# Cross-attention inside a two-layer decoder: the next context is requested at head 5 of a batch, and the totals are inverted in two halves at heads 11 and 13

## The chip, the cores and the metric

The kernel runs as one program on one core of a Trainium2 chip. Its time is the device time of one execution in microseconds (us). Three executions of the kernel before took 2054.67, 2056.34 and 2062.97 us, so the median is 2056.34 us. Five engines work side by side: TensorE (PE, with its weight loads shown apart as PEld), VectorE (DVE), ScalarE (ACT), GpSimd (POOL) and SyncE (SP), which here only issues DMAs. The 16 DMA engines of the core serve every queue.

## The reference, cut to what matters

The decoder has two layers. The change touches only the cross-attention of layer 0: 16 batches, 112 queries and 375 context rows each, 16 heads of width 16.

```python
q = x @ Wq + bq
kv = context @ Wkv + bkv
k, v = jnp.split(kv, 2, axis=-1)
# 16 heads of 16; both q and k are rotated by position
q = _larope(q, Lq)
k = _larope(k, Lk)
scores = jnp.einsum('bhqd,bhkd->bhqk', q, k) * SCALE
scores = jnp.where(context_mask[:, None, None, :], scores, -jnp.inf)
attn = jax.nn.softmax(scores, axis=-1)
out = jnp.einsum('bhqk,bhkd->bhqd', attn, v)
out = out.transpose(0, 2, 1, 3).reshape(B, Lq, H * hd)
return out @ Wo + bo
```

## The kernel before, in words

Every engine has its own instruction list, written by hand, and waits on semaphores. In the cross-attention stage each list is a loop over batches `b` and, inside a batch, over heads `h` from 0 to 15. Where a step stands in that loop fixes its place in its engine's order. `ahead(b, s, h + n, step)` runs a step for a head n places later, running over into the next batch; `s` is the parity of the batch and picks one of two buffers.

What one batch needs:

- **The context** of batch b+3 (375 KB) is loaded into one of three buffers by `load_context`, issued from ACT's queue. Before the change this happens in `copy_values`, at the third value copy, which stands at head 15. The buffer's last readers are the value matmuls (`values`, L1582), counted by `v_ready`.
- **Keys.** PE projects the keys of batch b+2 from its context at heads 0, 1, 2 and 4 (`keys`, L1571). DVE rotates them at heads 2, 3, 5, 6 (L1691), POOL adds and subtracts, and ACT casts three bf16 parts at heads 8, 12 and 14 (`cast_keys`, L1781). SP stores each part to DRAM (`store_parts`, L1444, 187.5 KB each). Then SP loads them back in the layout of the score matmul (`load_keys`, L1474): four loads of 187.5, 375, 562.5 and 375 KB; the last two wait for the third part's store. PE needs them for the first score of batch b+2, which stands at head 10 of batch b+1, since `scores` runs six heads ahead.
- **Scores and weights.** PE computes `scores(h+6)` (L1592), DVE biases them and takes their minimum, `bias_scores(h+4)` (L1703), ACT exponentiates, `exponentiate(h+3)` (L1786), PE transposes, `turn_probs(h+2)` (L1602), and DVE (L1709) or ACT (L1792) copies the result, `copy_probs(h+1)`. There are three buffers of scores, so `scores(n)` waits for `bias_scores(n-3)`. Every four heads PE weighs the values (L1618).
- **Totals.** The values' tile holds columns of ones, so the weighing gives the weighed sums and the total weights. ACT copies them at head 1 of the next batch (`copy_sums`, L1797), SP moves them with four DMAs (`move_sums`, L1483), which go behind `load_keys` on the same queue, DVE inverts the totals at head 12 (`invert`, L1714, semaphore `inverted`), and POOL multiplies (`scale_sums`, L1542).

In the first batches two more things run: ACT casts queries (L1817) and SP stores them (`store_queries`, L1454), in front of `move_sums`.

Of the kernel before, what the change touches and what calls it, by code (L numbers as in the profile page):

```python
# [24 lines left out]
B, L, D = 16, 112, 256  # L25
T = B * L
DH = D // P
# [1250 lines left out]
def cross_attention(k, g, ins):  # L1278
# [12 lines left out]
    with ExitStack() as ctx:  # L1291
# [27 lines left out]
        CK = S2 // KC  # L1319
# [4 lines left out]
        with ExitStack() as c2:  # L1324
# [20 lines left out]

            KEYS_AT, ROTATE_AT, CAST_AT = (0, 1, 2, 4), (2, 3, 5, 6), (8, 12, 14)
            VALUES_AT, COPY_VALUES_AT = (8, 9, 10, 11, 12, 13), (11, 13, 15)
            TURNED_BY_ACT = (1, 3, 5, 7, 8, 9, 11, 13, 15)
            TURNED_BY_DVE = tuple(h for h in range(NHEAD) if h not in TURNED_BY_ACT)

# [29 lines left out]
            def follows(b, n=1):  # L1380

                return not isinstance(b, int) or b + n < B

            def precedes(b):
                return not isinstance(b, int) or b > 0
# [47 lines left out]
            def load_context(queue, b):  # L1433
                queue.dma_start(context_of(b), ins["ctxT"][ds(b, 1)].rearrange("b (h p) t -> p (b h) t", p=P)).then_inc(ctx_loaded[b % len(contexts)], 16)
# [76 lines left out]
            @block.gpsimd  # L1511
            def _(pool):
                def sum_keys(b):
                    pool.wait_ge(k_read, b + 1)

                    wait(pool, k_cast, PARTS * b)
                    pool.tensor_tensor(key[:, 0], turn[:, 0], turn[:, 2], ALU.subtract)
                    pool.tensor_tensor(key[:, 1], turn[:, 1], turn[:, 3], ALU.add).then_inc(k_whole, 1)

                def lessen_keys(b, n):  # L1520

                    pool.wait_ge(k_cast, PARTS * b + n + 1)
                    pool.tensor_tensor(key[:], key[:], part[:, n], ALU.subtract).then_inc(k_less, 1)

                def lessen_queries(g_no, n):
                    pool.wait_ge(q_cast, PARTS * (g_no - 1) + n + 1)
                    pool.tensor_tensor(query_both(g_no), query_both(g_no), query_part(g_no, n), ALU.subtract).then_inc(q_less, 1)

                def turn_queries(g_no):

                    pool.wait_ge(q_kept, g_no - OTHERS)
                    for n, table in enumerate((q_cos, q_sin, q_sin, q_cos)):
                        last = pool.tensor_tensor(by_length(turned_query(g_no, n)), by_length(query(g_no, n // 2)), over_batches(table, g_no), ALU.mult)
                    last.then_inc(q_turned, 1)
                    pool.wait_ge(q_turned, g_no - OTHERS)
                    pool.tensor_tensor(query(g_no, 0), turned_query(g_no, 0), turned_query(g_no, 2), ALU.subtract)
                    pool.tensor_tensor(query(g_no, 1), turned_query(g_no, 1), turned_query(g_no, 3), ALU.add).then_inc(q_whole, 1)

                def scale_sums(b, s):

                    pool.wait_ge(inverted, b + 1)
                    pool.tensor_tensor(merged[:, :, chunk(b, L)], value_sum[:, s], power_sum[:, s], ALU.mult).then_inc(o_scaled, 1)  # L1542

                pool.memset(v[:], 1.0).then_inc(v_filled, 1)
                sum_keys(1)
                pool.wait_ge(q_whole, 2)
                for n in range(PARTS - 1):
                    lessen_keys(1, n)
                    lessen_queries(OTHERS, n)
                for b in range(B - 2):  # L1550
                    if b < NCH - 1:
                        turn_queries(OTHERS + 1 + b)
                    sum_keys(b + 2)
                    for n in range(PARTS - 1):
                        if b < NCH - 1:
                            lessen_queries(OTHERS + 1 + b, n)
                        lessen_keys(b + 2, n)
                    if b > 0:
                        scale_sums(b - 1, (b - 1) % 2)
                for b in range(B - 3, B):  # L1560
                    scale_sums(b, b % 2)
# [120 lines left out]
            def _(dve):  # L1682
# [25 lines left out]
                    dve.wait_ge(t_ready, NHEAD * b + h + 1)  # L1708
                    dve.tensor_copy(pt[:, h % PT_RING], turned_probs(h)).then_inc(pt_ready[0], 1)  # L1709

                def invert(b, s):

                    dve.wait_ge(o_moved[s], 16 * 4 * (b // 2 + 1))
                    dve.reciprocal(power_sum[:, s], power_sum[:, s]).then_inc(inverted, 1)  # L1714

                def batch(b, s):
                    for h in range(NHEAD):
                        ahead(b, s, h + 4, bias_scores)
                        if (h + 1) % NHEAD in TURNED_BY_DVE:
                            ahead(b, s, h + 1, copy_probs)  # L1720
                        if h == 12 and precedes(b):
                            invert(b - 1, 1 - s)
                        if follows(b, 2) and h in ROTATE_AT:
                            rotate_keys(b + 2, ROTATE_AT.index(h))

# [31 lines left out]
                    bias_scores(0, 0, h)  # L1757
                copy_probs(0, 0, 0)
                batches(dve, batch)
                invert(B - 1, 1)  # L1760

            @block.scalar
            def _(act):
                def copy_values(b, s, c):
                    if c == 0:

                        wait(act, pv_done, QUADS * (b - 1))
                    act.wait_ge(v_ready, CK * b + c + 1)
                    if c == CK - 1 and follows(b, 3):

                        load_context(act, b + 3)
                    act.activation(v[:, s, c, :, 0::2], value_ps(c).rearrange("p (h d) -> p h d", d=HD), ACT.Copy).then_inc(v_read, 1)

                def cast_keys(b, n):
# [19 lines left out]
                def copy_sums(b, s):  # L1794
                    act.wait_ge(pv_done, QUADS * (b + 1))
                    wait(act, o_moved[s], 16 * 4 * (b // 2))
                    act.activation(o_sb[:, s], o_ps[:, 0:QUADS * L].rearrange("p (r l) -> p r l", l=L), ACT.Copy).then_inc(o_copied, 1)  # L1797
# [28 lines left out]
                def batch(b, s):  # L1826
                    for h in range(NHEAD):
                        ahead(b, s, h + 3, exponentiate)
                        if b < NCH - 1 and h in CAST_QUERIES_AT:
                            cast_queries(OTHERS + 1 + b, CAST_QUERIES_AT.index(h))  # L1830
                        if (h + 1) % NHEAD in TURNED_BY_ACT:
                            ahead(b, s, h + 1, copy_probs)
                        if h == 1 and precedes(b):
                            copy_sums(b - 1, 1 - s)
                        if follows(b, 2) and h in CAST_AT:
                            cast_keys(b + 2, CAST_AT.index(h))
                        if follows(b) and h in COPY_VALUES_AT:
                            copy_values(b + 1, 1 - s, COPY_VALUES_AT.index(h))
# [1691 lines left out]
```

## Time and profile before

| | |
|---|---|
| median of three executions | 2056.34 us |
| the profiled execution's own time | 2056.47 us |
| its span | 2054.6 us |
| TensorE clock, mean of what was granted | 0.949 of full speed |
| PE busy | 1773.9 us, 86% |
| DVE busy | 1418.9 us, 69% |
| ACT busy | 1045.2 us, 51% |
| POOL busy | 1002.3 us, 49% |

The profile gives times in microseconds from the start of the span. A matmul is shown by its modelled end, so a full PE is not a PE at its peak. The loop over the batches of the cross-attention lies between about 533 and 822 us of the span; one batch takes some 17.5 us there once it runs evenly, and up to 21 us in the first ones.

### The profile page before, as it was taken

How to read it: one execution, taken by the hardware profiler on the slowest of the kernel's cores; microseconds unless marked ns; L12 is line 12 of the kernel's file. 1: busy time of each engine (PE TensorE's matmuls, PEld its weight loads, DVE VectorE, ACT ScalarE, POOL GpSimd, SP SyncE). 2: the span in 40 equal slices, each digit the busy share in tenths (PEclk: the TensorE clock that was granted, in tenths of full speed). 3: DMA queues.
4: the chain of work that ended last, by engine and by line, in shares of the span. 5: the costliest groups of instructions: out<-in, count | busy, mean ns of one | idle time of the engine just before them, and what ended most of it. 6: DMA issues, size and time to landing. Idle time of an engine off the chain costs nothing. (4 is left out here: it accounts for less than half of the span.)

```text
span 2054.6 us, 33436 instructions
## 1 busy us (share of the span) xinstructions
PE 1773.9 (86%) x11006; PEld 1107.5 (54%) x11006; DVE 1418.9 (69%) x2635; ACT 1045.2 (51%) x1948; POOL 1002.3 (49%) x756
## 2 busy tenths in 40 slices
PE   7967887889989999787888888888689989999799
PEld 4334444445667777443444444444554656665699
DVE  6779999993678888495555555554565348787893
ACT  4776667661788888336555554554323131114342
POOL 1269989881653321036566666665100009764342
PEclk9979999999999999899999989999899999999899
DMA  2034334433687774411556544633940044344640
GB/s 70 5 117 134 126 126 138 122 99 108 144 184 185 187 184 103 126 40 31 178 151 201 177 141 147 197 98 72 294 136 0 1 138 144 113 138 147 223 139 17
DMA packets 147377, 261.12 MB, mean 127 GB/s; under 512 B 39877, under 2 KB 104038, under 8 KB 144534
## 3 DMA queue, kind: packets, MB, share of 16 engines
q1 hardware_dynamic: 129846, 216.22, 35.7%
q0 software_dynamic: 13824, 37.77, 6.0%
q10 hardware_dynamic: 3536, 4.99, 0.9%
q8 instruction: 90, 1.47, 0.3%
q14 instruction: 81, 0.66, 0.1%
HBM read 205.82 MB, written 49.44 MB: 124 GB/s over the span
## 5 line engine op out<-in xcount | busy, mean ns | idle before, releaser
L3128 POOL DMA_INDIRECT moe_y<-ahead,moe_where x144 | 159.9, 1110 | 141.2 <-DVE ahead L3261 112.0
L3191 PE MATMUL moe_up_ps<-moe_w_tile,ahead 128*64 128x352 f32 x1152 | 214.3, 521 | 2.8 <-ACT moe_w_tile L3335 1.4
L2335 POOL TENSOR_TENSOR soft_power<-soft_logit,soft_high 128x1024 f32<-128x1024 f32 x28 | 66.2, 2363 | 289.3 <-DVE soft_high L2409 289.0
L3335 ACT ACTIVATE moe_w_tile<-moe_w 128x1216 f32 x144 | 175.4, 1219 | 24.1 <-issue 21.9
L3122 POOL DMA_INDIRECT ahead<-moe_tok,moe_where x144 | 144.2, 1001 | 56.9 <-issue 42.7
L1786 ACT ACTIVATE xattn_prob<-xattn_sm,xattn_least 112x375 f32<-112x375 f32 x256 | 150.8, 604 | 29.1 <-DVE xattn_least L1703 28.6
L1023 POOL TENSOR_TENSOR mamba_x_state<-mamba_x_state,mamba_cx_all 128x896 f32<-128x896 f32 x64 | 133.4, 2085 | 26.8 <-DVE mamba_x_state L1081 26.8
L3191 PEld LDWEIGHTS moe_up_ps<-moe_w_tile,ahead 128*64 128x64 f32 x1152 | 85.7, 153 | 103.1 <-issue 93.5
L1017 POOL TENSOR_TENSOR xn<-mamba_u,mamba_b_all 128x896 f32<-128x896 f32 x64 | 133.3, 2086 | 14.7 <-DMA mamba_b_all<-mamba_b 14.7
L1703 DVE CUSTOM_DVE_ANT_0 xattn_sm<-xattn_s_ps,wide 112x375 f32<-112x375 f32 x256 | 130.2, 539 | 13.0 <-PE xattn_s_ps L1592 9.7
L3255 DVE TENSOR_TENSOR moe_hid<-ahead,moe_up_ps 128x176 f32<-128x176 f32 x144 | 45.7, 333 | 133.9 <-ACT ahead L3341 82.5
L1081 DVE TENSOR_TENSOR_SCAN mamba_x_state<-xn,mamba_x_in 128x896 f32<-128x896 f32 x64 | 128.7, 2011 | 4.6 <-PE mamba_x_in L1116 4.6
L1602 PE MATMUL xattn_pt_ps<-ident,xattn_prob 112*125 112x112 f32 x768 | 126.7, 274 | 5.9 <-ACT xattn_pt L1792 3.8
L1602 PEld LDWEIGHTS xattn_pt_ps<-ident,xattn_prob 112*125 112x125 f32 x768 | 113.9, 189 | 31.5 <-issue 14.0
L1121 PE MATMUL mamba_y<-mamba_x_state,ident 128*128 128x448 f32 x256 | 108.1, 545 | 16.4 <-POOL mamba_x_state L1023 16.3
L980 ACT ACTIVATE mamba_scaled<-wide,mamba_b_turned 128x256 f32<-128x256 f32 x224 | 95.8, 495 | 48.7 <-PE mamba_x_in L1116 47.8
L3112 DVE COPY moe_w_tile<-moe_w 128x1216 f32 x144 | 109.1, 799 | 11.6 <-issue 11.6
L1121 PE MATMUL mamba_y<-ahead_small,ident 128*128 128x448 f32 x256 | 107.8, 544 | 0.0
L2359 PE MATMUL soft_lg<-soft_phi,xn 128*128 128x512 f32 x224 | 102.3, 600 | 4.4 <-PEq L365 4.4
L1116 PE MATMUL mamba_x_in<-ident,mamba_scaled 128*128 128x128 f32 x448 | 63.0, 282 | 49.6 <-ACT mamba_scaled L980 35.7
L2444 ACT ACTIVATE soft_power<-soft_power 128x1024 f32<-128x1024 f32 x28 | 29.6, 1058 | 149.1 <-POOL soft_power L2335 149.1
L2370 PE MATMUL soft_mix<-soft_tok,soft_share 128*128 128x256 f32 x448 | 101.2, 380 | 2.5 <-POOL soft_share L2340 1.3
(458 smaller groups left out, 4273.8 us busy)
## 6 DMA issues: line engine op xcount, KB each, us to landing
moe_w<-moe_w SPq DMA_DIRECT2D x64, 480.0 KB
soft_w<-soft_w SPq DMA_DIRECT2D x16, 1024.0 KB, 7.4
mamba_b_all<-mamba_b SPq DMA_DIRECT2D x32, 448.0 KB
mamba_cx_all<-mamba_c SPq DMA_DIRECT2D x32, 448.0 KB, 3.7
mamba_cy_all<-mamba_c SPq DMA_DIRECT2D x32, 448.0 KB, 4.5
moe_w_tile<-moe_y SPq DMA_DIRECT2D x14, 1024.0 KB, 8.1
soft_logits<-soft_logit SPq DMA_DIRECT2D x28, 512.0 KB, 2.6
soft_logit<-soft_logits SPq DMA_DIRECT2D x14, 1024.0 KB, 5.1
```

The costliest lines, as they stand in the source:

```text
L1017: pool.tensor_tensor(y_in[:, j % 2], u[:, c0 + j % 2, tok], b_all[:, n % 2], ALU.mult).then_inc(y_fed, 1)
L1023: pool.tensor_tensor(x_state[:, j % 2], x_state[:, j % 2], cx_all[:, n % 2], ALU.mult).then_inc(x_read, 1)
L1081: dve.tensor_tensor_scan(x_state[:, j % 2], x_decay[:, j % 2], x_in[:, 0:HW], 0.0, ALU.mult, ALU.add).then_inc(x_scanned, 1)
L1121: mm = pe.matmul(y[:, j % 2, w, 0:CW], g.ident[:], src[:, j % 2, w * CW:(w + 1) * CW], start=False, stop=False, skip_group_check=True)
L1602: mm = pe.transpose(turned_probs(h)[:, c], prob[:, h % RING, c * KC:(c + 1) * KC], g.ident[0:L, 0:L])
L1703: dve.tensor_tensor_reduce(sm[:, h % RING], s_ps[0:L, (NHEAD * b + h) % S_RING, 0:S2], mask[:, s], -SCALE, BIG, ALU.add, ALU.min, least[:, ...
L1786: act.activation(prob[:, h % RING], sm[:, h % RING], ACT.Exp, bias=least[:, s, h:h + 1], scale=-1.0).then_inc(p_ready, 1)
L3112: copy(w_tile[:, s, i, n:n + 1].rearrange("p a m -> p (a m)"), w[:, ds(e & (RING - 1), 1)].rearrange("p a m -> p (a m)")).then_inc(w_place ...
L3122: pool.indirect_dma_start(xg[:, 2 * s + i], None, tok_dram, bass.IndirectOffsetOnAxis(ap=where[:, 0, t:t + 1], axis=0)).then_inc(gathered[ ...
L3128: pool.indirect_dma_start(y_dram, bass.IndirectOffsetOnAxis(ap=where[:, 1, t:t + 1], axis=0), y_sb[:, 2 * s + i], None).then_inc(y_stored[ ...
L3191: mm = pe.matmul(up_ps[n * HALF:(n + 1) * HALF, i, 0:2 * I], xT[:, s % 2, at:at + HALF], w_tile[:, s, i, n, h * 2 * I:(h + 1) * 2 * I], st ...
L3335: place_weights = weight_placer(act, 0, lambda to, src: act.activation(to, src, ACT.Copy))
```

## The change: what it does

Two edits, both in the cross-attention.

1. The request for the context of batch b+3 leaves `copy_values` (head 15 of batch b-1, behind a cast of the keys) and stands at head 5 of batch b. In front of it ACT waits for all three value products of batch b, which were made in batch b-1. The load itself, its queue and its size stay.
2. The inversion of the totals becomes two operations on half of the columns each, one at head 11 and one at head 13, where one operation stood at head 12. The first half waits for the four DMAs of `move_sums`. `inverted` now counts two per batch, and POOL waits for both. After the last batch both halves follow one another.

```diff
+            CONTEXT_AT, INVERT_AT = 5, (11, 13)
...
-                    pool.wait_ge(inverted, b + 1)
+                    pool.wait_ge(inverted, DH * (b + 1))
...
-                def invert(b, s):
-
-                    dve.wait_ge(o_moved[s], 16 * 4 * (b // 2 + 1))
-                    dve.reciprocal(power_sum[:, s], power_sum[:, s]).then_inc(inverted, 1)
+                def invert(b, s, m):
+
+                    if m == 0:
+                        dve.wait_ge(o_moved[s], 16 * 4 * (b // 2 + 1))
+                    dve.reciprocal(power_sum[:, s, m], power_sum[:, s, m]).then_inc(inverted, 1)
...
-                        if h == 12 and precedes(b):
-                            invert(b - 1, 1 - s)
+                        if h in INVERT_AT and precedes(b):
+                            invert(b - 1, 1 - s, INVERT_AT.index(h))
...
-                invert(B - 1, 1)
+                for m in range(DH):
+                    invert(B - 1, 1, m)
...
-                    if c == CK - 1 and follows(b, 3):
-
-                        load_context(act, b + 3)
...
+                        if h == CONTEXT_AT and follows(b, 3):
+
+                            act.wait_ge(v_ready, CK * (b + 1))
+                            load_context(act, b + 3)
```

The line numbers below L1345 grow by one in the changed kernel. On DVE, heads 11 to 14 of one batch, before the change. ISA is the biasing of one head's scores with its minimum, COPY a `copy_probs`, TENSOR_SCALAR the next batch's mask, RECIPROCAL the inversion:

```order
L1709 COPY xattn_pt<-xattn_pt_ps 125x336
L1697 TENSOR_SCALAR wide<-ahead 112x375
L1703 ISA xattn_sm,xattn_least<-xattn_s_ps,wide 112x375
L1703 ISA xattn_least 112x1
L1714 RECIPROCAL ahead_small<-ahead_small 128x224
L1703 ISA xattn_sm,xattn_least<-xattn_s_ps,wide 112x375
L1703 ISA xattn_least 112x1
L1709 COPY xattn_pt<-xattn_pt_ps 125x336
```

The same place on DVE after the change:

```order
L1710 COPY xattn_pt<-xattn_pt_ps 125x336
L1716 RECIPROCAL ahead_small<-ahead_small 128x112
L1698 TENSOR_SCALAR wide<-ahead 112x375
L1704 ISA xattn_sm,xattn_least<-xattn_s_ps,wide 112x375
L1704 ISA xattn_least 112x1
L1704 ISA xattn_sm,xattn_least<-xattn_s_ps,wide 112x375
L1704 ISA xattn_least 112x1
L1710 COPY xattn_pt<-xattn_pt_ps 125x336
L1716 RECIPROCAL ahead_small<-ahead_small 128x112
```

The inversion, and with it the wait for the moved sums, now stands ahead of the mask and of the biasing of the next batch's first head; its second half follows the copy of head 14.

On ACT, heads 14 and 15 before the change. ACTIVATE `xattn_part` is the last key cast, `xattn_prob` an exponential, `xattn_v` the third value copy:

```order
L1781 ACTIVATE xattn_part<-xattn_key 128x750
L1786 ACTIVATE xattn_prob<-xattn_sm,xattn_least 112x375
L1434 DMA ahead<-ctxT 128x2x375
L1772 ACTIVATE xattn_v<-xattn_kv_ps 125x256
L1786 ACTIVATE xattn_prob<-xattn_sm,xattn_least 112x375
```

And on ACT after the change, heads 1 to 6 of the next batch, where ACTIVATE `ahead_small` is `copy_sums`:

```order
L1797 ACTIVATE ahead_small<-xattn_o_ps 128x448
L1786 ACTIVATE xattn_prob<-xattn_sm,xattn_least 112x375
L1792 ACTIVATE xattn_pt<-xattn_pt_ps 125x336
L1786 ACTIVATE xattn_prob<-xattn_sm,xattn_least 112x375 x2
L1792 ACTIVATE xattn_pt<-xattn_pt_ps 125x336
L1786 ACTIVATE xattn_prob<-xattn_sm,xattn_least 112x375
L1435 DMA ahead<-ctxT 128x2x375
L1786 ACTIVATE xattn_prob<-xattn_sm,xattn_least 112x375
L1792 ACTIVATE xattn_pt<-xattn_pt_ps 125x336
```

The request has moved from just behind the last key cast to the exponential at head 5.

## Rows read from the trace of the kernel before

**Rows 1.** Engines by stretch (busy us, count), TensorE clock, DMA share, GB/s.
```profile
core 0: us, PE busy (x) PEld busy (x) DVE busy (x) ACT busy (x) POOL busy (x), PEclk, DMA share, GB/s
650.00:670.00 20.00, 19.60 (x216) 15.25 (x217) 16.67 (x53) 17.86 (x40) 5.39 (x5) 1.00 0.82 198
```

**Rows 2.** Who waited for whom, 533 to 829: total us, times, longest.
```profile
DVE ahead_small L1714 <- DMA ahead_small<-ahead_small: 10.7, 4, 5.7
...
PE xattn_s_ps L1592 <- DVE xattn_least L1703: 7.6, 17, 2.0
...
PE xattn_s_ps L1592 <- DMA xattn_ks<-xattn_k_parts: 6.9, 9, 1.3
```

**Rows 3.** DMA issues in time, end of batch 11: start, duration, queue, line.
```profile
755.32 0.37 ACTq L1434 DMA_DIRECT2D ahead<-ctxT  x1
756.16 0.36 SPq L1444 DMA_DIRECT2D xattn_k_parts<-xattn_part  x1
760.22 0.77 SPq L1474 DMA_DIRECT2D xattn_ks<-xattn_k_parts  x2
```

**Rows 4.** DMA issues in time, end of batch 12, which requests no context.
```profile
774.59 0.36 SPq L1444 DMA_DIRECT2D xattn_k_parts<-xattn_part  x1
778.01 0.77 SPq L1474 DMA_DIRECT2D xattn_ks<-xattn_k_parts  x2
```

**Rows 5.** DMA view, 755 to 761: issue, count, KB, us to landing.
```profile
xattn_k_parts<-xattn_part SPq DMA_DIRECT2D x1, 187.5 KB, 4.0
```

**Rows 6.** The same view, 774.5 to 779.
```profile
xattn_k_parts<-xattn_part SPq DMA_DIRECT2D x1, 187.5 KB, 3.3
```

**Rows 7.** TensorE in time: first scores of three batches, with their idle time.
```profile
768.53 0.37 PE L1592 MATMUL xattn_s_ps<-xattn_ks,xattn_qs 128*112 128x375 bf16 x1 [1.27 <-DMA xattn_ks<-xattn_k_parts]
786.29 0.37 PE L1592 MATMUL xattn_s_ps<-xattn_ks,xattn_qs 128*112 128x375 bf16 x1 [0.61 <-DMA xattn_ks<-xattn_k_parts]
803.29 0.37 PE L1592 MATMUL xattn_s_ps<-xattn_ks,xattn_qs 128*112 128x375 bf16 x1 [1.14 <-DMA xattn_ks<-xattn_k_parts]
```

**Rows 8.** DMA view, 533 to 829: ACT's queue (packets, MB, share), then one issue.
```profile
q10 hardware_dynamic: 3264, 4.61, 6.0%
...
ahead<-ctxT ACTq DMA_DIRECT2D x8, 375.0 KB, 3.5
```

**Rows 9.** VectorE in time, batch 2, around the inversion.
```profile
587.20 0.79 DVE L1697 TENSOR_SCALAR wide<-ahead 112x375 f32<-112x375 uint8 x1
588.20 0.55 DVE L1703 CUSTOM_DVE_ANT_0 xattn_sm<-xattn_s_ps,wide 112x375 f32<-112x375 f32 x1 [0.21 <-DVE wide L1697]
590.76 1.55 DVE L1714 RECIPROCAL ahead_small<-ahead_small 128x224 f32<-128x224 f32 x1 [2.00 <-DMA ahead_small<-ahead_small]
592.23 0.49 DVE L1703 CUSTOM_DVE_ANT_0 xattn_sm<-xattn_s_ps,wide 112x375 f32<-112x375 f32 x1
```

**Rows 10.** TensorE in time: scores around the inversions of batches 1 to 3.
```profile
571.81 0.37 PE L1592 MATMUL xattn_s_ps<-xattn_ks,xattn_qs 128*112 128x375 bf16 x1 [0.94 <-DVE xattn_least L1703]
...
588.76 0.32 PE L1592 MATMUL xattn_s_ps<-xattn_ks,xattn_qs 128*112 128x375 bf16 x1
...
589.68 0.32 PE L1592 MATMUL xattn_s_ps<-xattn_ks,xattn_qs 128*112 128x375 bf16 x1
...
592.78 0.37 PE L1592 MATMUL xattn_s_ps<-xattn_ks,xattn_qs 128*112 128x375 bf16 x1 [2.02 <-DVE xattn_least L1703]
...
613.04 0.37 PE L1592 MATMUL xattn_s_ps<-xattn_ks,xattn_qs 128*112 128x375 bf16 x1 [1.63 <-DVE xattn_least L1703]
```

**Rows 11.** Instruction groups by shape: busy us, mean ns, idle before.
```profile
L1714 DVE RECIPROCAL ahead_small<-ahead_small 128x224 f32<-128x224 f32 x16 | 24.8, 1549 | 10.7 <-DMA ahead_small<-ahead_small 10.7
...
L506 DVE RECIPROCAL xattn_proj_out_ln_rstd<-xattn_proj_out_ln_rstd 128x112 f32<-128x112 f32 x4 | 3.4, 853 | 2.5 <-ACT xattn_proj_out_ln_rstd L502 2.5
```

**Rows 12.** Engines by stretch, batch 2, columns as in rows 1.
```profile
576.00:586.00 10.00, 9.51 (x96) 7.13 (x94) 8.37 (x27) 8.52 (x18) 6.29 (x6) 1.00 1.05 214
```

**Rows 13.** ScalarE in time, heads 3 to 6 of one even batch.
```profile
708.54 1.11 ACT L1786 ACTIVATE xattn_prob<-xattn_sm,xattn_least 112x375 f32<-112x375 f32 x2 [0.46 <-DVE xattn_least L1703]
```

## The prediction

> **What bounds the kernel now.** I read the engines by stretch first. In the even part of the cross-attention PE is busy 19.60 of 20 us, at the full granted clock, while the DMA engines are at 0.82 [rows 1]. So PE is nearly full; ACT and DVE follow at 17.86 and 16.67, and no change of order there can return more than PE's small holes. The list of waits names the holes: PE waited 6.9 us in nine places for the keys coming back from DRAM, and 7.6 us in 17 places for DVE's biased scores [rows 2]. Together that is 14.5 us, 0.7% of the span. Nothing in the diff lowers the work of PE, so this is the ceiling of a gain, and I look at each of the two holes by itself.
>
> The hole for the keys is a chain of DMAs: the third part is cast at head 14, stored, and only when it has landed do the last two loads go out; the first score of the next batch but one waits for them. In the batch that ends at 756 the store goes out at 756.16, the last loads at 760.22 [rows 3], and the score starts at 768.53 after 1.27 us idle [rows 7]: 12.37 us from store to score.
>
> The hole for DVE is mostly in batches 1 to 3. There the inversion waits for the moved sums: 2.00 us in batch 2 [rows 9]. The next biasing starts 592.23, and PE's score behind it at 592.78, after 2.02 us idle; batches 1 and 3 show 0.94 and 1.63 [rows 10]. These three are 4.6 of the 7.6 us.
>
> **The change part by part.** All is summed against the profiled execution's own time, 2056.47 us (1.9 above its span), which is 0.13 above the median of 2056.34.
>
> *The context request, what it leaves.* Before, it goes out 0.84 us ahead of the third store (755.32 against 756.16) [rows 3] and shares the DMA engines with it. Batch 12 asks for no context and is a control: its store lands in 3.3 us, where the one behind a context took 4.0 [rows 5, 6], the last loads follow after 3.42 us instead of 4.06, and store to score is 11.70 us (774.59 to 786.29) instead of 12.37 [rows 3, 4, 7]. So leaving this place is worth 0.67 us on the keys' chain.
>
> *Where it arrives.* At head 5 the ACT queue reaches it with the exponential that starts at 708.54 [rows 13] in a batch whose keys PE takes up near head 10, 5 us on. The keys' loads are then under way. One context costs 6.0% of 296 us over 12 requests, 1.48 us of all 16 engines [rows 8]. If all of it goes ahead of the last key, the keys are 1.48 us later. If the engines turn evenly between the two queues, much of it is left over when the keys are through, and at a share of 0.82 [rows 1] some 0.9 us of the 5 are free and take a part too, so that the cost may be near 0. The net on the keys' chain is then between -0.67 and +0.81 us per batch. I take the middle, a cost about equal to the 0.67 saved, and so zero; both ends stay for the range. There are nine even batches with a context (4 to 12): -6.0 to +7.3 us. PE feels a loss fully, since it already waits for the keys in most batches, and a gain only as far as it waits.
>
> ACT's added wait, for the values of this batch, is for products made in the batch before, so it holds nothing up; behind it are the exponential of head 9 and a copy. The context is used at head 0 of the next batch, 11 heads or some 12 us later, and a context lands in 3.5 us [rows 8]: hidden even if that triples.
>
> *The inversion in halves.* One operation of 128x224 takes 1.549 us, one of 128x112 0.853 [rows 11]; two are 1.71, so 0.16 us more per batch on DVE. DVE has 3 us and more free in 20 [rows 1], so in the middle this costs PE little; after the last batch nothing covers it: +0.16 us. What is better is that no block is longer than 0.85; against it, in even batches, the mask and first biasing of the next batch come 0.8 us later. Scores are made three ahead of the biasing, which is about one head, 0.92 us (588.76 to 589.68) [rows 10]. So this is covered with 0.1 us to spare if the sums have landed. Of 16 inversions only four wait today [rows 2], at head 12. At head 11 some more will, by 0 to 0.5 us. I take 0, with an upper bound of 0.4 x 9 = 3.6.
>
> *The inversion in batches 1 to 3.* Here the sums are late whatever DVE does, and the order decides. Let the sums land at L. Before, the biasing for the next batch's head 0 was done while waiting (588.20) [rows 9], and PE stood at the following score but one, which began at L + 2.02 (590.76 to 592.78). Now the mask and this biasing stand behind the first half: 0.85 + 0.79 + 0.21 + 0.55 [rows 9, 11], 2.4 us less 0.1 where operations overlap (the biasing at 592.23 starts 0.08 before the reciprocal's end at 592.31). The earlier score starts at L + 2.3 and the one that PE stood at one head later, L + 3.2. That is 1.2 us more in each, 3.6 us in three batches.
>
> L itself moves. From 576 to 586, where the context of head 5 now falls, the DMA engines are saturated (1.05) [rows 12], and the sums go out behind everything. The context adds its 1.48 us there; leaving its old place gives back what it held up there, 0.67, or 0.9 if all of its overlap is counted. I take +0.6 us each, 1.8 in all.
>
> Sum: 3.6 + 1.8 + 0.16 + 0 = +5.6 us, so 2056.5 + 5.6 = 2062.1; rounded 2062.
>
> **The rivals.**
>
> *Absorbed.* The three early stalls lie in batches where ACT also casts queries; a later wait takes up what is lost, and the keys' chain nets zero. For it: in such a batch ACT is busy 8.52 of 10 us and PE 9.51 [rows 12], so that a later stall could be behind ACT and not behind this one. Against: PE is idle exactly for DVE there [rows 10]. Time 2056.5.
>
> *Faster.* The saving of 0.67 us counts, and the context slips in beside the keys for nothing; the smaller blocks on DVE also spare PE its short waits. The nine waits for keys, 6.9 us [rows 2], fall: at 0.67 x 9 = 6.0 us, 2050.5. Against it: in batch 12, without any context, PE still waits 0.61 us, and the last one 1.14 [rows 7], so the waits do not go away when contention does.
>
> *Slower, past the bound.* The context goes ahead of the keys whole. The keys' chain is then 1.48 - 0.67 = 0.81 us longer in nine batches, +7.3, on top of the 5.6: 2069.4. It decides once a context holds up the keys by more than 0.67 us. For it: the DMA engines are at 0.8 already, and PE stands at the keys with no slack. It is the one that the skill's rule would make true.
>
> *The change does not do what it says.* The request could be held at head 5 by its new wait; the counts exclude it, and I give it nothing.
>
> **How the numbers follow.** Forecast 48%, absorbed 18%, faster 14%, slower past the bound 20%. The forecast's own range is 2057 to 2067. The range of 2051 to 2069 leaves out about half of the gain case and half of the slow one. A measurement of this kernel can tell about 0.5%, 10.3 us, from no change: faster means under 2046.1, which only an excess over the gain case reaches, 4%. Slower means over 2066.6: three quarters of the slow case and a tail of the forecast, 19%. The rest, 77%, is the same.
>
> **What would show each step.** In the profile after: the third store landing in about 3.3 us in every batch and the last loads 3.4 us behind it (leaving); the waits of the first scores for `xattn_ks`, 6.9 us in nine, near that if arrival and leaving cancel, 14 or so if the context goes first, under 2 in the gain case; the inversion's waits in batches 1 to 3 still 1 to 3 us, and PE's idle time for DVE there about 2 to 4 us each instead of 0.94 to 2.02; reciprocals of 0.85 us, 32 of them. I am wrong if these early stalls do not grow, or if inversions of even batches wait for sums by more than 0.5 us.

## The result and the profile after

The changed kernel takes 2069.4 us (median of 15 runs, 2061.64 to 2080.78) against 2058.68 of the kernel before in the same session (15 runs, 2054.0 to 2062.97). The ratio is 1.0055, interval 1.0037 to 1.0074: slower by 11.3 us. The forecast was 2062.0, with a range to 2069.0, so the direction is right and the time lies 0.4 us outside the range. The kernel before was itself 2.3 us above the median on which the forecast stood: of the added time, 5.6 us were forecast and 11.3 measured. Twice more, on other chips, the same kernel gave 1.0073 and 1.0082 (e5, e16 below). The loss is therefore nearer to 0.7% than to the 0.3% that I forecast.

The profiled execution has a span of 2072.7 us, 18.1 more than before; its time of 2074.48 us is above the median, so it shows more of the loss than a typical one. The cross-attention stage, from its first query projection to its last weighed sums, grew from 317.2 to 336.1 us, 18.9. The rest of the program changed by less than 1 us. So everything is to be looked for between 506 and 842 us.

Counted from third cast of keys to third cast, the periods of batches 1 to 3 grew from 60.3 to 67.8 us together, and the ten from batch 3 on from 177.5 to 189.2. The forecast had 5.4 us for the first group and nothing for the second.

The waits of the changed kernel in the batches (533 to 845 us): waiter, releaser, total us, count, longest.

```profile
PE xattn_s_ps L1593 <- DVE xattn_least L1704: 17.6, 26, 3.7
DVE ahead_small L1716 <- DMA ahead_small<-ahead_small: 17.5, 9, 4.4
PE xattn_s_ps L1593 <- DMA xattn_ks<-xattn_k_parts: 8.0, 5, 2.8
```

Against [rows 2], the wait for the keys barely moved (6.9 to 8.0 us, though in five places instead of nine). What grew is VectorE's wait for the moved sums. The 10.7 us of [rows 2] hold one wait of 5.7 after the last batch, at 826.62, which the window above leaves out (there it is 5.05, at 846.86); inside the batches it is 5.0 us in three places before and 17.5 in nine after. PE's wait for the biased scores behind it grew from 7.6 to 17.6 us: from 4.6 to 9.6 in batches 1 to 3 and from 3.0 to 8.0 in the even ones.

The timeline of the changed kernel in batch 1, the place that answers to [rows 9, 10] one batch earlier: start, duration, operation, idle time before it and what ended that.

```profile
572.78 0.85 DVE L1716 RECIPROCAL ahead_small<-ahead_small 128x112 f32<-128x112 f32 x1 [4.36 <-DMA ahead_small<-ahead_small]
573.55 0.29 DVE L1698 TENSOR_SCALAR wide<-ahead 112x375 f32<-112x375 uint8 x1
574.06 0.55 DVE L1704 CUSTOM_DVE_ANT_0 xattn_sm<-xattn_s_ps,wide 112x375 f32<-112x375 f32 x1 [0.21 <-DVE wide L1698]
574.67 0.56 PE L1593 MATMUL xattn_s_ps<-xattn_ks,xattn_qs 128*112 128x375 bf16 x1 [3.68 <-DVE xattn_least L1704]
```

Read it downwards: VectorE stands 4.36 us at the first half; the next batch's mask and first biasing are behind it, and PE stands 3.68 us for that biasing. Batches 2 and 3 show the same with 2.83 and 3.09 us; before the three were 0.94, 2.02 and 1.63 [rows 10].

This much was forecast. The next one, of an even batch, was not:

```profile
692.84 0.56 PE L1593 MATMUL xattn_s_ps<-xattn_ks,xattn_qs 128*112 128x375 bf16 x1 [2.80 <-DMA xattn_ks<-xattn_k_parts]
694.12 0.51 DVE L1710 COPY xattn_pt<-xattn_pt_ps 125x336 f32<-125x336 f32 x1 [3.90 <-PE xattn_pt_ps L1603]
696.23 0.85 DVE L1716 RECIPROCAL ahead_small<-ahead_small 128x112 f32<-128x112 f32 x1 [1.60 <-DMA ahead_small<-ahead_small]
700.17 0.37 PE L1593 MATMUL xattn_s_ps<-xattn_ks,xattn_qs 128*112 128x375 bf16 x1 [0.46 <-DVE xattn_least L1704]
```

PE first waits 2.80 us for the keys. The sums are moved behind the keys on SP's queue and are late too, so VectorE, now asked for them at head 11, waits 1.60 us more; PE loses 0.46 us to that at 700.17, much less than to the keys. Of the ten periods from batch 3 on, two take 22.0 us (this one, and one with 1.96 us for the keys and 2.85 for the sums), where before none took over 18.4. In both the mask takes 0.29 us, in both the context lands in 11.7 us and the last keys in 10.2 and 9.4. Why they land so late in these two batches and not in the others, no run shows.

Issues and landings of the changed kernel, between 677 and 687 us (KB each, us from issue to landing):

```profile
xattn_ks<-xattn_k_parts SPq DMA_DIRECT2D x2, 375.0 KB, 8.0
xattn_k_parts<-xattn_part SPq DMA_DIRECT2D x1, 187.5 KB, 3.5
```

```profile
ahead<-ctxT ACTq DMA_DIRECT2D x1, 375.0 KB, 11.7
```

The third store lands in 3.5 us, as forecast from [rows 5, 6]. But the context lands in 11.7 us where [rows 8] had 3.5, and the last two loads of keys in 8.0 (their median). Over the batches the median landing of a context is 6.6 us in the nine requests under one name of the buffer and 8.1 in the four under the other:

```profile
ahead<-ctxT ACTq DMA_DIRECT2D x9, 375.0 KB, 6.6
xattn_context<-ctxT ACTq DMA_DIRECT2D x4, 375.0 KB, 8.1
```

Windows of the changed kernel around the stall of batch 1 (after the busy times of PE, PEld, DVE, ACT and POOL: granted clock, DMA share, GB/s):

```profile
570.00:575.00 5.00, 1.32 (x8) 0.91 (x7) 2.00 (x5) 1.45 (x4) 2.78 (x2) 0.80 0.69 173
575.00:580.00 5.00, 5.00 (x39) 4.16 (x39) 3.58 (x13) 5.00 (x12) 3.66 (x4) 0.51 0.27 74
580.00:585.00 5.00, 5.00 (x50) 3.79 (x50) 3.61 (x11) 2.98 (x8) 3.60 (x4) 1.00 0.98 195
```

After the 3.68 us of idle time PE is granted 0.51, its lower level of 1.2 GHz, for some 5 us. The kernel before had in the same stretch:

```profile
575.00:580.00 5.00, 5.00 (x53) 3.79 (x50) 3.43 (x11) 4.16 (x10) 3.99 (x4) 1.00 1.08 245
```

The reciprocals took what was forecast, 32 of 0.844 us:

```profile
L1716 DVE RECIPROCAL ahead_small<-ahead_small 128x112 f32<-128x112 f32 x32 | 26.9, 844 | 22.6 <-DMA ahead_small<-ahead_small 22.6
```

### The profile page after: what moved, and what is told of

It reads as the page before. It is cut to its first block and busy times, and to the rows that moved or that the text cites. A ratio compares the mean times of both kernels' runs of the same rounds, so it can differ in the third digit from the quotient of the medians.

```text
span 2072.7 us, 33452 instructions
## 1 busy us (share of the span) xinstructions
PE 1782.6 (86%) x11006; PEld 1117.0 (54%) x11006; DVE 1420.8 (69%) x2651; ACT 1045.6 (50%) x1948; POOL 1003.7 (48%) x756
## 5 line engine op out<-in xcount | busy, mean ns | idle before, releaser
L1603 PEld LDWEIGHTS xattn_pt_ps<-ident,xattn_prob 112*125 112x125 f32 x768 | 120.0, 196 | 27.7 <-ACT xattn_prob L1786 12.0
L1593 PE MATMUL xattn_s_ps<-xattn_ks,xattn_qs 128*112 128x375 bf16 x256 | 89.2, 350 | 28.4 <-DVE xattn_least L1704 18.1
```

The costliest lines, as they stand in the source:

```text
L1603: mm = pe.transpose(turned_probs(h)[:, c], prob[:, h % RING, c * KC:(c + 1) * KC], g.ident[0:L, 0:L])
```

## The experiments

All ratios are to the kernel before on the same chip, with their 95% interval; e1 to e4, e5 to e8, e9 to e12 and e13 to e16 each shared one. The kernel before took 1984.3, 2049.6, 2051.1 and 1985.6 us on these four, so a comparison across groups is one of ratios. "The stage" is the stretch named above, from the profiled execution. Where I speak of even batches in numbers, it is the sum of the ten periods from batch 3 on, as above.

### Which part, and does the low clock matter? (e1 to e4)

e1 keeps the request at head 5 and undoes the halves (shown against the changed kernel):

```
-                        if h in INVERT_AT and precedes(b):
-                            invert(b - 1, 1 - s, INVERT_AT.index(h))
+                        if h == 12 and precedes(b):
+                            invert(b - 1, 1 - s)
```

> Only the context request moves to head 5; the inversion stays whole at head 12. Theory 1 (the request at head 5 delays the keys and the moved sums, which stand behind the keys on the same queue): most of the loss is here, 5 to 9 us over the kernel before; the inversion of batches 1 to 3 waits about 0.6 us longer each than the 0.92, 2.00 and 2.05 before. Theory 2 (the place of the first half ahead of the next batch's first biasing makes the loss): at most 3 us over before.

Measured: 1.0019 (1.0002 to 1.0036), 3.8 us; the stage is 323.6 us. The inversions of batches 1 to 3 wait 1.96, 0.23 and 4.04 us, against 0.92, 2.00 and 2.05 before: 1.3 us more in all, though not 0.6 each.

e2 keeps the halves and puts the request back:

```
-                        if h == CONTEXT_AT and follows(b, 3):
-                            act.wait_ge(v_ready, CK * (b + 1))
-                            load_context(act, b + 3)
+                    if c == CK - 1 and follows(b, 3):     (in copy_values)
+                        load_context(act, b + 3)
```

> Only the inversion is split, at heads 11 and 13; the context request stays at head 15. Theory 2: PE's idle time for the biased score in batches 1 to 3 grows by about 1.2 us each, to 2 to 3.2 us, the granted clock falls behind each, and the time is 4 to 8 us over before. Theory 1: within 3 us of before.

Measured: 1.0063 (1.0038 to 1.0088); the stage is 334.7 us. The halves carry nearly the whole loss.

e3 is e2 with the halves one head later:

```
-            CONTEXT_AT, INVERT_AT = 5, (11, 13)
+            CONTEXT_AT, INVERT_AT = 5, (12, 14)
```

> The inversion is split, but its first half stands at head 12, where the whole one stood, and the second at head 14; the context request stays at head 15. Theory 2 (the order, not the splitting, costs): the same as before within 2 us, perhaps 1 to 2 us faster since the block is shorter; PE's stalls of batches 1 to 3 are 0.7 us shorter each. If splitting itself costs (0.16 us of VectorE per batch), 1 to 3 us over before.

Measured: 0.9968 (0.9953 to 0.9984), faster than before. So it is not the splitting that costs, it is the place: one head is 0.95%. The gain of 6.3 us is more than the 1 to 2 that I expected, and the fifteen periods of its profile are only 1 us shorter than those of the kernel before, so where the rest comes from is not shown.

e4 is the changed kernel, in which PE runs twelve spare products of 60 columns in the stall of batches 1 to 3:

```
+                        if h == 13 and b in (1, 2, 3):
+                            for n in range(FILL):
+                                pe.matmul(spare, g.mean_w[:], g.mean_w[:, 0:60], start=True, stop=True)
```

> The changed kernel with 12 extra matmuls of 60 columns, whose result nothing reads, in each of batches 1 to 3, in front of the score at head 13, where PE stood idle for 2.8 to 3.7 us. Theory 3 (these idle times make the granted clock fall to half for the stretch behind them, and that costs 1.5 to 2.5 us each on top of the wait): the granted clock stays 1.00 between 575 and 630 and the time is 4 to 7 us below the changed kernel's. Without that theory the extra work lies in a wait and the time is the changed kernel's, or up to 2 us more.

Measured: 1.0052 (1.0028 to 1.0076). Its windows over the same stall:

```profile
570.00:575.00 5.00, 3.92 (x29) 3.29 (x28) 4.70 (x14) 2.98 (x6) 2.19 (x3) 1.00 0.47 121
575.00:580.00 5.00, 5.00 (x53) 3.68 (x55) 3.30 (x12) 4.52 (x11) 4.92 (x6) 1.00 0.62 138
```

The clock stays at 1.00 in these ten us, and of the windows of 5 us up to 630 only 595 to 600 is lower, at 0.66; the changed kernel has 0.51, 0.69, 0.62 and 0.66 in four of them. The time does not settle the theory. It asked for 4 to 7 us less than the changed kernel, 0.2 to 0.35%; the changed kernel gave 1.0055, 1.0073 and 1.0082, but never on this chip, and with the interval of e4 both no gain and this one are possible.

### Which batches? (e5 to e8)

> The changed kernel itself, so that the other kernels of this group have it beside them. It took 1.0055 of the kernel before. Theory 1 and 2 alike: 1.004 to 1.008 of before again. If the two parts simply add, the sum of what each took alone, 1.0019 and 1.0063: 1.008.

Measured: 1.0073 (1.0048 to 1.0097).

e6 is the changed kernel with `INVERT_AT` at (12, 14), so e3 with the request at head 5.

> The changed kernel, but with the halves at heads 12 and 14 instead of 11 and 13; the context request stays at head 5. Theory 2 (the first half stands one head too early): most of the loss goes, and what is left is that of the context request less the gain of the halves at 12 and 14, 0.9968 x 1.0019, so 0.998 to 1.001 of before. Theory 1: 1.004 or more.

Measured: 0.9984 (0.9967 to 1.0001). Against e3 (another chip) the request costs 0.16%, as in e1.

e7 and e8 are e2 with

```
+                        invert_at = (11, 13) if b <= 3 else (12, 14)     (e7)
+                        invert_at = (11, 13) if b > 3 else (12, 14)      (e8)
```

> Context request at head 15 as before. The halves stand at heads 11 and 13 in batches 1 to 3 and at 12 and 14 in the others. Theory 4 (the loss of the early half is made in the batches where the moved sums are late, with the halved clock behind it): nearly all of the loss, 5 to 9 us over before. If it is made in the even batches: the same as before or faster.

> Context request at head 15 as before. The halves stand at heads 12 and 14 in batches 1 to 3 and at 11 and 13 from batch 4 on. Theory 4: within 3 us of before. If the even batches carry the loss too, as waits for the sums of 0.3 to 1.2 us in some of them let expect: 4 to 9 us over before.

Measured: e7 1.0011 (0.999 to 1.0031), e8 1.004 (1.0019 to 1.0061). Against e3's 0.9968 (another chip) head 11 costs 0.43% in batches 1 to 3 and 0.72% in the even ones. The larger half of the loss lies where I had put nothing.

What happens in one of the three slow even batches (21.1 to 21.2 us), in the timeline of e8:

```profile
723.88 0.37 PE L1593 MATMUL xattn_s_ps<-xattn_ks,xattn_qs 128*112 128x375 bf16 x1 [1.74 <-DMA xattn_ks<-xattn_k_parts]
726.26 0.85 DVE L1716 RECIPROCAL ahead_small<-ahead_small 128x112 f32<-128x112 f32 x1 [1.07 <-DMA ahead_small<-ahead_small]
726.83 1.51 POOL L1524 TENSOR_TENSOR xattn_key<-xattn_key,xattn_part 128x750 f32<-128x750 f32 x1 [3.30 <-ACT xattn_part L1785]
727.03 1.51 DVE L1698 TENSOR_SCALAR wide<-ahead 112x375 f32<-112x375 uint8 x1
728.76 0.55 DVE L1704 CUSTOM_DVE_ANT_0 xattn_sm<-xattn_s_ps,wide 112x375 f32<-112x375 f32 x1 [0.21 <-DVE wide L1698]
729.37 0.37 PE L1593 MATMUL xattn_s_ps<-xattn_ks,xattn_qs 128*112 128x375 bf16 x1 [1.62 <-DVE xattn_least L1704]
```

Three delays follow one another: late keys (1.74 us), behind them late sums (1.07), and the mask, which takes 1.51 us instead of 0.29 to 0.35 and ends 0.20 after the GpSimd operation that started 0.20 before it. PE waits 1.62 us for the biasing. Something else happens one batch earlier in the same profile:

```profile
708.96 0.84 DVE L1716 RECIPROCAL ahead_small<-ahead_small 128x112 f32<-128x112 f32 x1
709.72 0.49 DVE L1704 CUSTOM_DVE_ANT_0 xattn_sm<-xattn_s_ps,wide 112x375 f32<-112x375 f32 x1
709.78 0.82 ACT L1785 ACTIVATE xattn_part<-xattn_key 128x750 bf16<-128x750 f32 x1
710.33 0.37 ACTq L1435 DMA_DIRECT2D ahead<-ctxT  x1
710.70 0.36 SPq L1445 DMA_DIRECT2D xattn_k_parts<-xattn_part  x1
```

```profile
xattn_k_parts<-xattn_part SPq DMA_DIRECT2D x1, 187.5 KB, 6.7
```

The second half stands at head 13, ahead of the biasing for which the exponential in front of the request waits. So the request goes out 0.37 us ahead of the third store, where before it was 0.84 [rows 3]. VectorE did not wait for the sums in this batch.

The store lands in 6.7 us instead of 4.0 [rows 5], and the next keys, at 723.88, are late. The waits of e8 against those of e6:

```profile
DVE ahead_small L1716 <- DMA ahead_small<-ahead_small: 13.6, 9, 5.1
PE xattn_s_ps L1593 <- DMA xattn_ks<-xattn_k_parts: 12.6, 10, 1.7
PE xattn_s_ps L1593 <- DVE xattn_least L1704: 12.5, 25, 1.7
```

```profile
DVE ahead_small L1716 <- DMA ahead_small<-ahead_small: 11.9, 6, 5.1
PE xattn_s_ps L1593 <- DVE xattn_least L1704: 7.3, 16, 2.6
PE xattn_s_ps L1593 <- DMA xattn_ks<-xattn_k_parts: 4.8, 6, 2.0
```

Both tables hold the wait of 5.1 us after the last batch. It looked as if the delays became a cycle: late sums, late biasing, a late request, and with it late keys of the next batch. e10 below speaks against its first link. And the changed kernel requests the context at head 5, where its third stores land in 3.1 to 3.5 us, so this way to late keys is one of e2 and e8 and not of the changed kernel.

### Is it the wait for the sums? (e9 to e12)

> Context request at head 5, the halves at heads 12 and 13: the first behind the next batch's first biasing, the second only one biasing later. Theory 5 (what costs in the even batches is that the wait for the moved sums stands in front of the mask and the next batch's first biasing, so that PE stops at the score of head 13): 0.996 to 1.000 of before, like the halves at 12 and 14. If it is the second half at head 13 that costs: 1.003 or more.

Measured for (12, 13), request at head 5: 0.9994 (0.9976 to 1.0012). It differs from the changed kernel in the place of the first half alone, and the loss of 0.55 to 0.82% is gone: what costs there is a first half ahead of the next batch's mask and first biasing, and not the second half at head 13.

e10 is e2 with the halves at 11 and 13 taken from a tile of ones, so that VectorE never waits for the sums; GpSimd waits for them where it scales. VectorE waits instead for the scaling two batches back and for its own last inversion (these lines are left out here):

```
-                    if m == 0:
-                        dve.wait_ge(o_moved[s], 16 * 4 * (b // 2 + 1))
-                    dve.reciprocal(power_sum[:, s, m], power_sum[:, s, m]).then_inc(inverted, 1)
+                    dve.reciprocal(stand_in[:, s, m], stand_in[:, s, m]).then_inc(inverted, 1)
```

> Halves at heads 11 and 13, context request at head 15, as in the kernel that took 1.0063 of before; but both halves work on a tile of ones instead of the moved totals, so VectorE does not wait for the sums. What it leaves out: the division by the totals. The operations, their sizes and places stay; GpSimd waits for the sums instead. Theory 5: VectorE no longer stops, PE has no idle time of over 0.5 us for a biased score, and the time is 6 to 12 us below that kernel's, so 0.997 to 1.001 of before. Rival (the order itself costs, sums or no sums): 1.004 or more.

Measured: 0.9998 (0.9985 to 1.0011), against 1.0063 for e2. With the same operations in the same order and VectorE's wait for the sums gone, e2's loss of 0.63% is gone from the whole. (e2 ran on another chip.) That does not settle each part, though. Its waits:

```profile
PE xattn_s_ps L1596 <- DMA xattn_ks<-xattn_k_parts: 15.0, 13, 3.3
PE xattn_s_ps L1596 <- DVE xattn_least L1707: 4.4, 16, 0.9
```

PE now waits for the keys instead, 15.0 us, and so e10 is not faster than e3. In this profile batches 1 to 3 take 56.1 us, where e2 took 64.1 and the kernel before 60.3. But the even batches take 186.2 us, against 190.9 in e2 and 177.5 before: without any wait for the sums they keep most of the excess. The request is as late as in e8 and the stores land as late:

```profile
669.79 0.37 ACTq L1436 DMA_DIRECT2D ahead<-ctxT  x1
670.15 0.36 SPq L1446 DMA_DIRECT2D xattn_k_parts<-xattn_part  x1
```

```profile
xattn_k_parts<-xattn_part SPq DMA_DIRECT2D x1, 187.5 KB, 6.9
```

In every even batch of e2, e8 and e10 whose request the traces hold, it stands 0.33 to 0.44 us ahead of the third store, against 0.84 before. So e10 shows that the wait costs in batches 1 to 3. For the even batches it leaves a rival: that, with the request at head 15, the second half at head 13 delays the request. The expected limit was missed too: PE's longest wait for a biased score is 0.95 us, behind a mask of 1.66.

e11 is the kernel before with the whole inversion at head 11:

```
-                        if h == 12 and precedes(b):
+                        if h == 11 and precedes(b):
```

> One whole inversion, only moved from head 12 to 11, context request at head 15. Theory 5: it loses what the halves at 11 and 13 lose or more, since the block behind the sums is 0.7 us longer: 1.005 to 1.010 of before. If the splitting is what costs: 1.002 or less.

Measured: 1.0034 (1.0011 to 1.0056), less than the 1.005 to 1.010 expected. The place costs without any splitting; here the request stands 1.15 us ahead of the third store, so it costs without a late request too.

> Context request at head 5, the halves one head later still, at 13 and 15. Theory 5: the sums have landed in the even batches, and in batches 1 to 3 PE's stall moves one head on and shrinks by about 1 us each: 1 to 4 us below the kernel with halves at 12 and 14, 0.996 to 0.998 of before. A rival price: GpSimd scales the sums later, which nothing waits for. If the place no longer matters: 0.998 to 1.000.

Measured for (13, 15), request at head 5: 0.9977 (0.9957 to 0.9996). With e3 it is the version that beats both kernels.

### How much of it is the mask? (e13 to e16)

e13 is e8, e14 the changed kernel, with the next mask made ahead of the first half and no longer in front of the biasing of head 0:

```
+                        if h == 11 and follows(b, 1):
+                            make_mask(b + 1, 1 - s)
                         if h in INVERT_AT and precedes(b):
                             invert(b - 1, 1 - s, INVERT_AT.index(h))
```

> Halves at heads 11 and 13 from batch 4 on, at 12 and 14 in batches 1 to 3, the context at its old place, as in e8; new: the mask of the next batch is made at head 11, ahead of the first half, where VectorE waits for the sums anyway. Theory (the stretched mask starts the slow batches of 21.1 us): all masks take under 0.8 us, the slow batches go, and the ratio to before falls from the 1.004 of e8 to 1.000 or less. Rival (the mask is only its own price, 2.5 us in 15 batches, and the late sums and the late store set the rest): the masks are short all the same, but the ratio falls by 0.12% at most, to 1.0028 or more, and batches over 20 us stay.

> The changed kernel with the mask made at head 11 ahead of the first half. In batches 1 to 3 the biasing behind the first half comes 0.3 us sooner, three times, 0.9 us; in the even batches two masks of 1.4 us fall to 0.3, 2.2 us. Theory (the mask starts slow batches): a ratio of 1.003 or less, against 1.0055 and 1.0073 for the changed kernel. Rival (its own price only): 3 us, 0.15%, so 1.004 to 1.006.

> The kernel of e8 once more, control for e13 on this chip: 1.004 (1.002 to 1.006) expected by every theory.

> The changed kernel once more, control for e14 on this chip: 1.004 to 1.008 expected by every theory.

Measured: e13 1.002 (1.0 to 1.0039), beside it e15 1.0035 (1.0017 to 1.0052); e14 1.0039 (1.0019 to 1.006), beside it e16 1.0082 (1.0055 to 1.0109). In e14 every mask is under 0.81 us and the longest even period is 18.8; in e16 three masks take 1.01 to 1.30 us and two periods 20.8 and 20.6. Batch 1 of e14:

```profile
572.67 0.85 DVE L1720 RECIPROCAL ahead_small<-ahead_small 128x112 f32<-128x112 f32 x1 [3.04 <-DMA ahead_small<-ahead_small]
573.44 0.49 DVE L1708 CUSTOM_DVE_ANT_0 xattn_sm<-xattn_s_ps,wide 112x375 f32<-112x375 f32 x1
573.99 0.56 PE L1593 MATMUL xattn_s_ps<-xattn_ks,xattn_qs 128*112 128x375 bf16 x1 [2.52 <-DVE xattn_least L1708]
```

The biasing starts 0.77 us behind the half's start, where it took 1.28 in the changed kernel (572.78 to 574.06). PE's waits for the biasing are 14.1 us in e14 and 20.7 in e16 (500 to 860 us):

```profile
PE xattn_s_ps L1593 <- DVE xattn_least L1708: 14.1, 23, 3.8
```

```profile
PE xattn_s_ps L1593 <- DVE xattn_least L1704: 20.7, 32, 4.5
```

The difference e14 to e16 is 0.43%, 8.5 us, and with both intervals it can be anything from 0.1 to 0.8%. The 0.15% of the rival lies within that, and e14's 1.0039 misses the 1.003 of the theory and stands by the 1.004 of the rival. So the place of the mask costs something in the changed kernel; that it costs more than its own duration is not shown. Against it speak the two slow batches of the changed kernel's profile, whose masks take 0.29 us, and the second slow period of e16, which has a short mask too. For the even batches alone (e13 to e15) the difference of 0.15% is within the intervals. e15 lost 0.35% in time although its profile shows no stretched mask in the even batches, which take 181.2 us, where the profile of the same kernel as e8 had three stretched masks and 190.6. A single profile thus tells which delays exist, but is off by nearly 10 us on how often they come.

## Why the prediction missed

- *Which hole.* That the change could return little and that the inversion's order was the risk was right. So was the sign.
- *Batches 1 to 3, +3.6 and +1.8.* Right in mechanism: the stalls of 3.68, 2.83 and 3.09 us lie within the 2 to 4 that I named, 5.0 us above the 4.6 of before [rows 10], and the three periods grew by 7.5 us where the two terms are 5.4. Timed by itself in e7, the order costs 0.43% (8.8 us) against e3, but only 0.11% above the kernel before, since the halves at 12 and 14 gain 0.32% by themselves (e3). My sum lies between.
- *Even batches, "covered with 0.1 us to spare if the sums have landed", "I take 0, with an upper bound of 0.4 x 9 = 3.6".* This is the step that failed. e8 and e15 lose 0.40% and 0.35% against before, 8.2 and 7.0 us, and 0.7% against e3; in the profile of the changed kernel the even batches are 11.7 us longer. The condition was the weak point. I read from [rows 2] that four of 16 inversions wait at head 12; it is three, since the fourth stands after the last batch. And I took the margin of the others as given, though I had only shown that it is above zero at head 12. The trace of before had it. The mask starts where a half at head 11 would; for one even batch, the last move of the sums, the mask, and the time to landing:

```profile
710.92 0.63 SPq L1483 DMA_DIRECT2D ahead_small<-ahead_small  x1
715.55 0.34 DVE L1697 TENSOR_SCALAR wide<-ahead 112x375 f32<-112x375 uint8 x1
```

```profile
ahead_small<-ahead_small SPq DMA_DIRECT2D x1, 56.0 KB, 5.2
```

The sums land at 716.10, 0.55 us after the mask has started. Over the eleven batches from 628 to 805 us they land between 0.86 us before it and 0.55 after, in five of them after. So there was no margin. After the change six of these inversions wait 0.39 to 2.85 us, which is the sign of being wrong that I had named. Where PE stands for the keys, the sums behind them on SP's queue are often late too: after the key waits at 654, 693, 766 and 787 us VectorE waited 0.85, 1.60, 2.85 and 1.21 us, in e8 after five of nine. I also treated each wait as a term by itself, 0 to 0.5 us. That the first half's place ahead of the mask and the first biasing is what costs is shown by e9. By what way it costs in the even batches is not: PE's waits for the biasing grew there by 5.0 us and for the keys by 1.1, which leaves about half of the 11.7 us, and two stretches at half the clock, from 692.5 and 767.6 us, have no price by any run.
- *The mask's price.* I took 0.79 us from [rows 9] for three batches, and no other number. That row was itself a stretched one: it takes 0.29 to 0.35 in most batches, and 1.38 and 1.39 in two batches of the changed kernel, where it starts just behind GpSimd's subtraction of the parts. Behind the second of them PE waited 1.64 us for the biasing. e14 puts some of the loss there, with the size open.
- *Leaving head 15, 0.67 us.* Right for the store, which lands in 3.1 to 3.5 us in each batch. The gain did not reach PE, whose wait for the keys went from 6.9 to 8.0 us.
- *Arrival at head 5, net zero, between -6.0 and +7.3 us.* Roughly right: e1 has +3.8 us (0.4 to 7.1), e6 against e3 0.16%. The third rival has the right direction here, but its time of 2069.4, which the measurement repeats to the digit, was built on +7.3 for the context and nothing for the even inversions. The agreement is a coincidence; e1 and e2 split the loss the other way.
- *The halves after the last batch, +0.16.* Right in size: two of 0.84 us.
- *Absorbed, faster.* Neither happened.

The Trainium skill, "DMA: Bandwidth & Descriptors", section "Queues, rings and completion order", says that a DMA engine drains a whole packet of one queue before it turns to the next; from this I had worked out that the context passes ahead of waiting keys in one turn. The landings at 677 to 687 us show contention (3.5 to 11.7 us), but in such a batch it is the context that waits too. The 7.3 us of that rival are just above the interval of e1, whose whole loss is 0.4 to 7.1 us.

What stays open: how the loss of the even batches divides between late sums, late keys, the stretched mask and the low clock, and, in e2, e8 and e15, the request that goes out late. e13 against e15 did not resolve it. The changed kernel with its wait for the sums taken out, which would, was not run; e10 has the request at head 15.

## What to carry to other kernels

A wait moved one step earlier is priced by the margin with which its data arrives in each turn of the loop, not by whether it waited where it stood; read when the data landed, and what is queued behind the waiting instruction. Where several loads share a queue, one late transfer makes the next late as well, so that these waits come together and cannot be counted one by one. Look also at what issues behind the moved step: a half of 0.84 us in front of one biasing moved a request 0.4 to 0.5 us nearer to the store with which it shares the DMA engines. To split a long operation is worth more if its first part stays behind the work for which another engine stands: at heads 12 and 14 the same halves gained 0.3% that at 11 and 13 lost 0.6.

## What the runs showed of the hardware

The mask, 112x375 from uint8 to fp32, takes 0.29 to 0.35 us, but longer where it starts beside a running GpSimd TENSOR_TENSOR of fp32. In the 18 traces 44 masks take 0.43 to 1.84 us, and each of them ends 0.21 us after a GpSimd operation that had started before it; where the mask starts first it keeps its short time (657.30 in the changed kernel, 0.29 us, GpSimd 0.02 behind). Least, median and greatest ns of the 15 masks between 540 and 845 us, and the time from the first to the last, in the changed kernel:

```profile
L1698 DVE TENSOR_SCALAR wide<-ahead x15: 290/291/1394, 550.5 to 825.4; 112x375 f32<-112x375 uint8 x15
```

and in e8:

```profile
L1698 DVE TENSOR_SCALAR wide<-ahead x15: 291/293/1512, 548.9 to 817.8; 112x375 f32<-112x375 uint8 x15
```

This agrees with the Trainium skill, "SBUF — State Buffer", section "Who interferes with whom": a VectorE tensor_scalar can run in a mode that takes the pair of ports it shares with GpSimd, and whichever of the two comes second is then blocked while the first runs. In e8 the mask began 0.20 us after the GpSimd operation and ended 0.20 after it.

PE's granted clock fell to 0.5 after an idle time of 2.80 us too. One-us windows of the changed kernel:

```profile
692.00:693.00 1.00, 0.16 (x1) 0.17 (x2) 0.00 (x0) 0.32 (x1) 0.00 (x0) 0.76 1.04 230
693.00:694.00 1.00, 1.00 (x5) 1.00 (x6) 0.00 (x0) 0.00 (x0) 0.00 (x0) 0.50 1.10 217
```

Whether the low clock costs time there is open: e4 removed most of it in batches 1 to 3, and its time is compatible with no gain and with the 4 to 7 us of the theory.
